# Last causal attention of a four-layer block: score products on 32-row tiles of the array, one copy of the keys, other places for the sums and the side products, other banks

## The reference

```python
def _L3_attn_ref(x, W1, b1, W2, b2):      # 16 heads of 8 features
    y = jnp.einsum('bse,ef->bsf', x, W1) + b1
    y = y.reshape(B, S, H, -1).transpose(0, 2, 1, 3)
    q, k, v = jnp.split(y, 3, axis=-1)
    dk = jnp.asarray(v.shape[-1], x.dtype) ** 0.5
    w = jnp.einsum('bhqd,bhkd->bhqk', q, k) / dk
    mask = jnp.tril(jnp.ones((S, S), dtype=x.dtype))
    w = w * mask - NEG_BIG * (1.0 - mask)
    w = jax.nn.softmax(w, axis=-1)
    attn = jnp.einsum('bhqk,bhkd->bhqd', w, v)
    attn = attn.transpose(0, 2, 1, 3).reshape(B, S, E)
    return jnp.einsum('bse,ef->bsf', attn, W2) + b2
...
    x = x + s * g      # s: this attention, g: silu of the last feed-forward
```

## Time and profile before

| | us |
|---|---|
| median of three runs | 1697.95 |
| profiled execution, device time | 1706.63 |
| its span, first to last instruction | 1704.9 |
| busy in the span: PE, weight loads, DVE, ACT, POOL | 1490.4, 1197.3, 1260.4, 1089.9, 857.1 |

### The profile page before, as it was taken

The page is one execution under the profiler, slowest core; times in us unless marked ns, Lnnn a source line. Parts: engine busy times, 40 slices in busy tenths (PEclk is TensorE's granted clock), DMA queues, the critical chain, the costliest instruction groups (busy, mean ns, idle before and its releaser), DMA issues. The chain is left out here.

```text
span 1704.9 us, 29946 instructions
## 1 busy us (share of the span) xinstructions
PE 1490.4 (87%) x11248; PEld 1197.3 (70%) x11248; DVE 1260.4 (74%) x2770; ACT 1089.9 (64%) x2122; POOL 857.1 (50%) x798
## 2 busy tenths in 40 slices
PE   6999999999999999899848888845999379998997
PEld 4788887888788887687737676834788256666675
DVE  6999999999999999435461677589433887777772
ACT  4888888888888888455445565632444456666665
POOL 4556576667666666720363744624666632233211
PEclk9999999999999999999779999957999699999999
DMA  3656666656666565300044000040465200000000
GB/s 94 124 103 115 106 120 100 120 108 114 115 108 103 99 105 106 87 1 1 18 137 129 26 2 2 2 133 1 112 148 109 64 1 1 2 2 2 2 2 26
DMA packets 334417, 117.09 MB, mean 69 GB/s; under 512 B 281008, under 2 KB 326096, under 8 KB 334144
## 3 DMA queue, kind: packets, MB, share of 16 engines
q1 hardware_dynamic: 323664, 101.54, 29.2%
q0 software_dynamic: 8496, 12.59, 3.4%
q10 hardware_dynamic: 2112, 1.05, 0.2%
HBM read 37.53 MB, written 10.49 MB: 28 GB/s over the span
## 5 line engine op out<-in xcount | busy, mean ns | idle before, releaser
L2135 ACT ACTIVATE ET_a<-PS 128x256 f32<-128x256 f32 (+2 forms) x512 | 220.5, 499 | 114.8 <-PE PS L2028 72.9
L771 POOL TENSOR_TENSOR dl<-XN,dh 128x1024 f16<-128x1024 f32 x86 | 184.9, 2150 | 155.2 <-DVE D L743 79.7
L205 PE MATMUL PS<-xh,yh 128*128 128x512 f32 x512 | 215.5, 421 | 6.6 <-ACT XNT L608 3.8
L206 PE MATMUL PS<-xl,yh 128*128 128x512 f32 x512 | 204.0, 398 | 0.0
L207 PE MATMUL PS<-xh,yl 128*128 128x512 f32 x512 | 202.8, 396 | 0.0
L608 ACT ACTIVATE G<-PS,nm 128x1024 f32<-128x1024 f32 x128 | 143.0, 1117 | 53.4 <-DVE nm L693 37.9
L608 ACT ACTIVATE XNT<-PS,nm 128x1024 f32<-128x1024 f32 x128 | 143.1, 1118 | 52.3 <-DVE nm L693 41.0
L687 DVE TENSOR_REDUCE nm<-PS 128x1 f32<-128x1024 f32 x128 | 156.6, 1223 | 15.7 <-PE PS L207 13.8
L689 DVE TENSOR_REDUCE nm<-PS 128x1 f32<-128x1024 f32 x128 | 156.0, 1219 | 4.7 <-PE PS L207 1.0
L205 PE MATMUL PS<-dth,xnh 128*128 128x256 f16 x512 | 141.0, 275 | 12.0 <-DVE zl L697 12.0
L2323 DVE CUSTOM_DVE_ANT_0 PS<-PS,mk 128x256 f32<-128x256 f32 (+3 forms) x256 | 128.2, 516 | 30.6 <-PE PS L2007 30.2
(11 more groups left out here) (461 smaller groups left out, 4091.1 us busy)
## 6 DMA issues: line engine op xcount, KB each, us to landing
e_wg<-in_WgT SPq DMA_DIRECT2D x16, 256.0 KB
e_wu<-in_WuT SPq DMA_DIRECT2D x16, 256.0 KB
e_wd<-in_WdT SPq DMA_DIRECT2D x16, 256.0 KB
dth<-dh SPq DMA_TRANSPOSE x128, 3.2
dtl<-dl SPq DMA_TRANSPOSE x128, 3.2
m_x_rows<-m_xs SPq DMA_DIRECT2D x1, 1472.0 KB, 4.9
m_xs<-m_x_rows SPq DMA_DIRECT2D x5, 256.0 KB, 4.8
m_y_rows<-m_xs SPq DMA_DIRECT2D x5, 256.0 KB, 2.3
```

Source lines behind the costliest of these rows:

```text
L205: e.matmul(o, l[0], r[0], start=start, stop=False)
L206: e.matmul(o, l[0], r[1], start=False, stop=False)
L771: e.tensor_tensor(self.dl[:, g % 4, :], self.D[g % 3], self.dh[:, g % 4, :], SUB).then_inc(*self.d_low.up(g))
L2135: e.activation(dst, src, ACT.Exp, scale=self.SC, bias=0.0).then_inc(*self.ex.up(it))
```

## The change

- The keys of a quad are kept once, `KA[:, n % 3, :]`. A score product takes the head's own 32 partitions of `QS` and `KA` and goes to a tile of 32 rows of the array (`tile_position=(32 * hh, 0)`). The spreading of keys on ACT and POOL is gone, and DVE writes the keys straight to `KA`.
- `lag` is 70: col j of head x stands at the same step as row j of head x + 5. Steps 12 and 13 hold no scores. In a step the row now comes before the col.
- The sums stand at steps 4 and 10, and part 0 waits for the first triangle alone; ACT takes bank 6 out at step 12 instead of 6.
- Side products use banks 7 and 5 in turn. Rows keep three banks, cols have two (3, 4); before the cols begin the rows have five, after the last row the cols three.
- "max" stands at steps 1 and 5, "project" at step 1 and 8 of the second head of a quad, 0 of the third and 1 of the fourth, "give" at step 8.
- The row parts come in another order: the four narrow ones, then the left parts mixed with the right parts. The small minimum (L2328) is gone: the right part's masked reduction starts from the left part's maximum, a value per partition read from `P2`, and waits for it.

```diff
-        self.KH = [[sb(f"KH{n}_{i}", [128, 1024], F32R) for i in range(4)] for n in range(3)]
+        if kind == 3:
+            self.KA = sb("KA", [128, 3, 1024], F32R)
...
+            self.rparts += [firsts[0], firsts[1], seconds[0], firsts[2], seconds[1], firsts[3], seconds[2], seconds[3]]
...
-        self.AV_AT = (0, 4) if kind == 3 else (11, 12)
-        self.lag = 63 if kind == 3 else 70
+        self.AV_AT = (4, 10) if kind == 3 else (11, 12)
+        self.lag = 70
...
-        sides = (7,) if kind == 3 else (7, 5)
+        sides = (7, 5)
...
-        rs, cs, rn, cn = list(range(3 if kind == 1 else 6)), [], 0, 0
+        rs, cs, rn, cn = list(range(3 if kind == 1 else 5)), [], 0, 0
...
-                rs, cs, rn, cn = [0, 1, 2], [3, 4, 5] if kind == 3 else [3, 4], 0, 0
+                rs, cs, rn, cn = [0, 1, 2], [3, 4], 0, 0
...
-                cs, cn = list(range(4 if kind == 3 else 3)), 0
+                cs, cn = list(range(3)), 0
...
-                t = e.matmul(o[:, 0:wd], qs[:, 128 * i:128 * i + 128], kh[:, c0:c0 + wd], start=True, stop=True)
+                r = slice(32 * hh, 32 * hh + 32)
+                t = e.matmul(o[:, 0:wd], qs[r, 128 * i:128 * i + 128], kh[r, c0:c0 + wd], start=True, stop=True, tile_position=(32 * hh, 0))
...
-                t = e.matmul(o[:, 0:wd], kh[:, 128 * jj:128 * jj + 128], qs[:, q1 - wd:q1], start=True, stop=True)
+                r = slice(32 * hh, 32 * hh + 32)
+                t = e.matmul(o[:, 0:wd], kh[r, 128 * jj:128 * jj + 128], qs[r, q1 - wd:q1], start=True, stop=True, tile_position=(32 * hh, 0))
...
-                q.wait_ge(self.cut, (x, 1))
+            q.wait_ge(self.cut, (x, part if self.kind == 3 else 1))
...
+            if self.kind == 3 and j in self.at and x < self.NH:
+                row(x, self.at[j])
             if m in self.at and 0 <= y < self.NH:
                 col(y, self.at[m])
-            if j in self.at and x < self.NH:
+            if self.kind == 1 and j in self.at and x < self.NH:
                 row(x, self.at[j])
...
+                    least = 3e38
+                    if c0:
+                        least = self.P2[:, n % 2, i - 4, hh:hh + 1]
+                        q.wait_ge(self.top, ("row", x, self.rparts.index((i, 0, c0, True))))
                     e.tensor_tensor_reduce(out=o[:, 0:c1 - c0], in0=o[:, 0:c1 - c0], in1=w.mk[:, 512 - (c1 - c0):512], scale=-1.0,
-                                           scalar=3e38, op0=ADD, op1=MIN, accum_out=dst).then_inc(*self.top.up(it))
-                if j == self.nr - 1:
-                    m4 = M[:, 4:8, col].rearrange("p i c -> p (i c)")
-                    q.wait_ge(self.top, it)
-                    e.tensor_tensor(m4, m4, self.P2[:, n % 2, :, hh], MIN).then_inc(*self.top.up(("both", x)))
+                                           scalar=least, op0=ADD, op1=MIN, accum_out=dst).then_inc(*self.top.up(it))
```

More of the change, by code:

```diff
@@ L1646, in __init__ @@
         self.scratch = None if kind == 3 else self.ET[1][:, :, :].rearrange("p j w -> p (j w)")[:, 0:1024]
-        self.KH = [[sb(f"KH{n}_{i}", [128, 1024], F32R) for i in range(4)] for n in range(3)]
+        if kind == 3:
+            self.KA = sb("KA", [128, 3, 1024], F32R)
+        else:
+            self.KH = [[sb(f"KH{n}_{i}", [128, 1024], F32R) for i in range(4)] for n in range(3)]
         edge = 64 if kind == 1 else 0
@@ L1702, in __init__ @@
             if hh == 0 and 1 <= n <= self.NQ:
-                m += [("max", n - 1, c) for c in range(2)]
-            if n + 1 < self.NQ and hh in (1, 2):
-                m += [("project", n + 1, w_, hh - 1) for w_ in (1, 0)]
+                m += [(1, ("max", n - 1, 0)), (5, ("max", n - 1, 1))]
+            if n + 1 < self.NQ:
+                m += {1: [(1, ("project", n + 1, 1, 0)), (8, ("project", n + 1, 0, 0))], 2: [(0, ("project", n + 1, 1, 1))],
+                      3: [(1, ("project", n + 1, 0, 1))]}.get(hh, [])
             if x - 7 >= 1 and (x - 7) % 2 and x - 7 < NH:
-                m += [("give", x - 7)]
+                m += [(8, ("give", x - 7))]
             if x in (33, 35):
-                m += [("fin", (x - 33) // 2), ("finp", (x - 33) // 2)]
+                m += [(1, ("fin", (x - 33) // 2)), (4, ("finp", (x - 33) // 2))]
             elif x in (34, 36):
-                m += [("sum", (x - 34) // 2)]
-            for j, what in enumerate(m):
-                self.misc[x, 1 + 3 * j] = what
+                m += [(2, ("sum", (x - 34) // 2))]
+            for j, what in m:
+                self.misc[x, j] = what
         first = [("project", 0, w_, ck) for w_, ck in ((1, 0), (0, 0), (1, 1), (0, 1))]
@@ L1772, in __init__ @@
         self.row = k.sig("a_row", rows)
-        self.top = k.sig("a_row_max", [y for r in rows for y in ([r] + ([("both", r[1])] if kind == 3 and r[2] == self.nr - 1 else []))])
+        self.top = k.sig("a_row_max", rows)
         self.col = k.sig("a_col", cols)
@@ L1941, in maxima @@
             _, n, c = u
-            q.wait_ge(self.top, ("both", 4 * n + 3) if self.kind == 3 else ("row", 4 * n + 3, self.nr - 1))
+            q.wait_ge(self.top, ("row", 4 * n + 3, self.nr - 1))
             o = k.bank(self.side_of[u])
@@ L2108, in spread @@
                 q.wait_ge(self.mi, u)
-                for hh in heads:
+                for hh in (0, 2):
                     r = slice(32 * hh, 32 * hh + 32)
                     self.k_free(q, n, hh)
-                    to, own = self.KH[n % 3][hh][:, 512 * ck:512 * ck + 512], k.cst("block")[:, hh:hh + 1]
-                    if self.kind == 3:
-                        e.activation(to, f(hn), ACT.Copy, scale=own).then_inc(*self.k_act.up(("k", n, ck, hh)))
-                    else:
-                        e.activation(to[r, :], f(hn[r, :]), ACT.Copy).then_inc(*self.k_act.up(("k", n, ck, hh)))
+                    to = self.KH[n % 3][hh][:, 512 * ck:512 * ck + 512]
+                    e.activation(to[r, :], f(hn[r, :]), ACT.Copy).then_inc(*self.k_act.up(("k", n, ck, hh)))
         def col(x, j):
@@ L2166, in act @@
                 col(y, self.at[m])
-            if j == (6 if self.kind == 3 else 13) and 0 <= x - 6 < self.NH and x % 2:
+            if j == (12 if self.kind == 3 else 13) and 0 <= x - 6 < self.NH and x % 2:
                 take_out(x - 6)
@@ L2200, in hm_free @@
         _, n, w_, ck = u
-        if w_:
+        if w_ and self.kind == 1:
             q.wait_ge(self.k_act, ("k", n, ck, 2))
```

54 lines of the change are left out of this document (19 added, 35 removed).

## The result

| | before | after |
|---|---|---|
| median of four runs each, us | 1697.53 | 1826.35 |
| lowest and highest | 1695.24, 1697.96 | 1817.84, 1831.42 |
| profiled execution, device time | 1706.63 | 1831.42 |
| its span | 1704.9 | 1829.6 |

A forecast was written before the change was run, and what follows sets the result against it. PE was taken to bound the middle stage, and after the change PE, two col banks and ACT. Middle -27.3, first and last +0.6 each: -26 from 1697.95 gives 1672, plus 2 for waits 1674 us; range 1648 to 1697.

The forecast's parts named there:

- Score products on 32-row tiles: Last attention: a row and its col on different strips cost only the longer product, 1.6 us less per head.
- rival D: PE's clock falls in the middle stage: 4.4 us per head, 119 over 27 heads, 1720 us at 40%; chance 0.10.
- the ring: Middle stage: PE, two col banks and ACT wait for each other and set 7.94 us per head without side products.
- Overlap: Row and col products of one step run side by side on different strips, saving 1.6 us per head.
- A: The sum of the forecast's terms holds: 1674 us, within 1660 to 1685; chance 0.55.
- Rival C: No overlap of row and col, or dearer changes of tiles: 0.6 us per head, 16 us, giving 1690; chance 0.18.
- First and last stage: Stages with rows only, and with cols and sums only: each 0.6 us longer, from 39.7 and 33.2 us.
- The change of tile: On PE, each change between score products and sums or side products costs 0.11 us.
- PE's own work: PE's work in a middle-stage head without side products: 5.1 of 7.94 us, with 2.45 for pairs of score products.
- B: DVE rules the middle stage: 31.5 us per quad, 209 for the stage, 1645 in all; chance 0.12.
- Keys kept once: ACT loses 2.7 us per quad and a wait of 1.6, POOL its copies; no term of its own.
- Minimum folded in: DVE saves 0.26 us per head without the small minimum; starting reductions from a value per partition costs 0.

The follow-up runs named there:

- e2: The kernel before with only its score products put on 32-row tiles; key copies, order and banks untouched: 1839.65 us, ratio 1.0762.
- e1: The changed kernel with score products over all 128 rows of the single keys, so each score sums four heads: 1697.89 us, ratio 0.9932.
- e5: The changed kernel with score products on tiles of 64 rows, so each score sums two heads: 1722.13 us, ratio 1.0078.
- e12: The kernel before plus eleven stretches of 200 products on PE alone, whole, 32-row, 64-row or alternating: whole products took 0.228 us each.
- e7: e1 with three banks for cols in place of two and one for side products: 1686.45 us, ratio 0.9868.
- e3: The changed kernel without the tiles and the single keys: whole-row score products on four key copies, new order, two col banks: 1740.07 us, ratio 1.0175.
- e10: e3 with three banks for cols in place of two and one for side products: 1692.71 us, ratio 0.9979.
- e4: The changed kernel with every score product on rows 0 to 31, so no two overlap: 1893.3 us in one run.

## Why the prediction was wrong

**The step that failed** is "Score products on 32-row tiles". It priced tiles by columns at the full clock and left the clock to rival D with 0.10. D gave two reasons, a PE emptied to 65% and products that fill a quarter of the array. The argument against it, that PE "was held as loosely" from 1368 to 1384 us at 1.00, met the first alone, and it was the second that counted. The step itself noted that no row of the trace had such tiles: this unknown touched all of PE's work and deserved far more than 0.10, and a range that reached D's price. What the runs showed in its place: the tiles by themselves, in the old order, bring the clock to 0.57 and the time to 1.0762 (e2), and the rest of the change without them gives 0.9932 (e1).

**D's price was right,** and in the head looked at so was its path, the ring with PE at 1.2 GHz: 4.4 us per head, 119 over 27 heads. After's middle stage is 115.4 us longer than e1's (369.0 against 253.6), 4.3 per head. A head without side products was 7.94 + 3.4 (2.2 for the sums, 1.2 for the products) = 11.3 by it, and the last one measured 11.98. What it lacked is the share: nearly all of the stage, where 40% was taken, and the last stage as well, which grew by 23.5 where it was given nothing.

**Overlap** held as a fact, and not as a gain. e5 overlaps where two heads lie in different halves of the array, which is so for two of a quad's four heads, at full clock in its quad from 1488.41 us: 38.51 us, where e1, with no overlap, takes 38.06 from 1490.12:

```profile
1488.41:1526.92 38.51, 36.20 (x414) 23.76 (x413) 30.57 (x92) 25.33 (x56) 5.10 (x8) 1.00 0.01 2
```
```profile
1490.12:1528.18 38.06, 36.25 (x414) 26.80 (x413) 30.57 (x93) 25.45 (x55) 5.09 (x8) 1.00 0.01 2
1627.54:1636.36 8.82, 8.63 (x97) 5.75 (x96) 6.43 (x21) 5.87 (x13) 1.27 (x2) 1.00 0.01 2
```

The 0.6 per head between A and C, 1.2 us for two heads, did not show. The forecast's quad of 35.4 (four times 7.94 and 3.6) was 2.7 too short by e1. What tiles of 32 rows would give at full clock, no run of the whole kernel shows; an order in which products of four heads stand together, as e12's four strips, was not tried.

**Rival C** described e1 well: 8.54 for a head without side products (8.82 in the second row above), and 1690 in all, where 0.9932 of 1697.95 is 1686. **First and last stage** of e1, 40.35 and 35.77, stand beside the forecast 40.3 and 33.8 ("39.7 + 0.6" and "33.2 + 0.6").

**The ring** held: e7's 11 us. **The change of tile** was priced at 0.11. In e12's alternation each product brings one change and starts 0.43 after the last, 0.20 over 0.228. The cost lies on both sides of a change: in e5 the three products of a projection between tiles start at 1490.42, 1490.76 and 1490.99, and the row behind them at 1491.32, so the last costs 0.33 as the first costs 0.34. The forecast counted the side behind the change. **PE's own work** has a slip: 5888 columns at 0.23 per 512 are 2.65 us and not 2.45, so 5.3 of 7.94 or 67%, and B's quad of 31.5 should be 31.0 (29.0 and four times 0.5), which its 209 us go by; the forecast does not hang on either. **Keys kept once** "stands in no term of its own". e3 against e1 puts it at 42 us with two col banks, part of it by the clock, and e10 against e7 at 19 (0.9979 against 0.9868) with three, of which moving ACT's copies gave back 15; the forecast named the mechanism, a shorter hold of ACT, and counted it inside the 3.6 per quad. **Minimum folded in** was forecast as 0.26 us less of DVE per head and gave nothing: DVE is busy for 202.20 us over 27 heads in e1's middle stage and for 201.99 over 27.5 before, 7.5 against 7.3 per head. The starts from `P2` took it back, with two more reductions per head in a place behind a read.

## What to carry to other kernels

Before packing small products into tiles of the array, ask what share of its rows they fill over time, and whether the form changes between them: here 32-row tiles between other work put nearly all of the stage at half rate. Where a trace lacks the resource that a change rests on, measure it by itself first, as e12 did in one run, or let the range hold its worst price. With few banks between two engines, put the engine's odd jobs where its partner issues nothing for it: that and a third bank brought e3 from a ratio of 1.0175 to 0.9896.

## What the runs showed of the hardware that was not expected

- A single 32-row strip with PE busy all the time has 1.2 GHz (clock 0.50, e12 and e4); four strips in turn have 2.4 GHz and start 0.058 us apart, 3.9 times the rate of whole products. The Trainium skill ("TensorE: Matmul & The Clock Gate", Part 3, "Measured speedup vs the span model") has 3.07 for four row tiles of 512 columns; over 200 products in a row, each with new weights, it was 3.9 here.
- 64-row tiles keep 1.00 by themselves and 0.95 in the kernel's middle stage (e5), with 0.50 from 1394 to 1414 us.
- Zeros count as much as other values for the clock: whole products with zeros in 96 of 128 rows have 0.99 (the kernel before), with none 1.00 (e1).
- Standing still lowers the clock with whole products too: behind a wait of 2.61 us one ran at the lower clock (e3, 1533.47), and e3's middle stage has 0.92.
- Alternating whole and 32-row products start 0.43 us apart at full clock and 0.72 at the lower one (2105.70 less 2104.97 is 0.73), and the clock falls, though most of the rows are in use.
- A masked reduction on DVE that starts from a value per partition takes some 60 ns more than one that starts from a constant in the same place (483 against 420 at 256 columns, 617 against 560 at 384), and one right behind a read of the accumulator some 40 more than one behind a `tensor_reduce`.
